# Reordering the third feed-forward ring and taking the best sums from four bands of candidates

## The chip, the cores and the metric

The kernel runs on one core of a Trainium2 chip. Its time is the device time of one execution in microseconds; lower is better. The engines are TensorE (PE, with its weight loads as PEld), VectorE (DVE), ScalarE (ACT), GpSimd (POOL) and SyncE (SP, which issues the transfers). Each has its own queue, in which instructions go in order; semaphores order work between queues.

## The reference

Four transformer layers, each an attention and a feed-forward part, over 2048 rows of width 128. The change touches the feed-forward part of the second layer, a lookup among experts by product keys:

```python
x = inputs.reshape(b * s, d)
xn = (x - x.mean(axis=0)) * rsqrt(x.var(axis=0) + EPS) * bn_gamma + bn_beta
q = (xn @ w_q.T).reshape(b, s, 2, NH, KD)...         # NH = 8 heads, KD = 128
sim = einsum('pbnhd,hkpd->pbnhk', q, keys_p)          # two lists of NK = 32 a head
scores, idx = top_k(sim, K)                           # K = 8 best of each list
all_scores = (scores[0][..., :, None] + scores[1][..., None, :]).reshape(..., K * K)
all_idx = ...
sc, pk = top_k(all_scores, K)                         # 8 best of 64 sums
indices = take_along_axis(all_idx, pk)
hmid = sigmoid(sc) * gelu(einsum('bnd,bnhkd->bnhk', inputs, down[indices]))
return einsum('bnhk,bnhkd->bnd', hmid, up[indices])
```

Both lists of eight are sorted, the largest first.

## The kernel before

The lookup is computed densely. There are 32 x 32 = 1024 possible experts, so for a tile of 128 rows and a head the kernel adds every similarity of list one to every one of list two (1024 sums), and keeps the sigmoid of a sum where the sum is at least the eighth best. These gates, turned and summed over the 8 heads, weight a dense product with all experts.

There are 16 tiles of 128 rows (`TILES`). Each passes through a ring over 8 heads, head h of tile i being step n = 8i + h:

- POOL, `pool1`: the 1024 sums of a head (`pairsum`, four buffers, so product n waits for gate n-4). Line 1669.
- ACT, `step` in `scalar1`: the sigmoid of the sums into PSUM (two buffers, `sig_bank`, so it waits for gate n-2). Line 1643. After the sigmoid of head 3 it does three other things for later tiles: `inputs` (the normalized rows of tile i+3), `copy_sims` (the similarities of tile i+2 out of PSUM, line 1625), `lowered` (gelu of the expert inputs of tile i+1 in two halves, line 1633, with a table load before and one after it).
- VectorE, `step` in `vector1`: the gate, `(pairsum >= eighth best) * sigmoid` (`gated`, four buffers, line 1741). In between: `mix` (turned gates times gelu, tile i-1, line 1726) after the gate of head 1, `tops` (16 MAX8 over 32 similarities, tile i+1, line 1701) after heads 2 and 3, `combine` (64 sums for each of 8 heads, one instruction, line 1706) and `add_tile` (line 1731) after head 3, `bests` (8 MAX8 over 64 sums, line 1717) after heads 5 and 6.
- TensorE, `step` in `tensor1`: 8 transposes of the gates of a head, summed over the heads in PSUM (line 1571). In between: `upper(i-1)` after head 0 (16 matrix products in the profile, line 1561), `similar(i+2)` after head 1 (line 1547), both halves of `lower(i+1)` after head 3 (line 1552).

`similar` and the first half of `lower` share bank 6, `upper` and the second half of `lower` share bank 7; the waits that this needs are in the code. `steps1` runs the tiles: the first four and the last four written out, the eight in the middle in a loop over groups of four. In the call of a step, `first` tells how many tiles came before and `last_` how many come after. `own_wait` is a memset of one element on VectorE.

Of the kernel before, what the change touches and what calls it, by code (L numbers as in the profile page):

```python
# [25 lines left out]
P = 128  # L26
# [3 lines left out]
TILES = TOKENS // P  # L30
# [1210 lines left out]
NE_USED = 1024  # L1241
CHUNKS = NE_USED // P
PK_HEADS, NK, TOPK = 8, 32, 8
EXPERTS = 8
CAPACITY = 640


def feed_forward(nc, ctx, sb, sem, S, w):
# [25 lines left out]
    xbT = QT[:, 2, :].rearrange("p (a b) -> p a b", a=2)  # L1274
    sims = OT[:].rearrange("p a b -> p (a b)").rearrange("p (g n) -> p g n", g=4)
    top = sb("top", [P, 2, 16, TOPK])
    combos = QT[:, 4:6, :].rearrange("p a b -> p (a b)")
    best = sb("best", [P, 2, PK_HEADS, TOPK])
    pairsum = KM[:].rearrange("p a b c -> p (a b c)").rearrange("p (r n) -> p r n", r=4)
    gated = both[:].rearrange("p (r n) -> p r n", r=4)  # L1280
# [252 lines left out]
    def tensor1(pe, A):  # L1533
# [31 lines left out]
        def step(first, last_, i, t):  # L1565
            for h in range(PK_HEADS):
                pe.wait_ge(gated_ready, PK_HEADS * i + h + 1)
                if h == 0 and first > 0:
                    pe.wait_ge(mixed, 2 * i)
                for c in range(CHUNKS):  # L1570
                    last = pe.matmul(weight_bank(c), gated[:, h % 4, c * P:(c + 1) * P], ident[:],  # L1571
                                     is_transpose=True, start=(h == 0 and c % 4 == 0),
                                     stop=(h == PK_HEADS - 1 and c % 4 == 3), skip_group_check=True)
                last.then_inc(wT_done, 1)
                if h == 0 and first > 0:

                    pe.wait_ge(act_ready[1], 2 * i + 2)
                    upper(i - 1, t - 1)
                if h == 1 and last_ > 1:

                    pe.wait_ge(act_ready[1], 2 * i + 1)
                    similar(i + 2, t)
                if h == 3 and last_ > 0:

                    if last_ > 1:
                        pe.wait_ge(sims_ready, i + 3)
                    lower(i + 1, 0)
                    if first > 0:
                        pe.wait_ge(added[1], i)
                    lower(i + 1, 1)  # L1590
# [7 lines left out]
        lower(0, 1)  # L1598
        steps1(pe, step)
        prepare_tensor(pe)  # L1600
        upper(TILES - 1, TPG - 1)
        prepare_tensor_end(pe)

    def scalar1(act, A):
# [31 lines left out]
        def step(first, last_, i, t):  # L1636
            for h in range(PK_HEADS):
                n = PK_HEADS * i + h
                act.wait_ge(sum_ready, n + 1)
                if first > 0 or h >= 2:  # L1640

                    act.wait_ge(gated_ready, n - 1)
                act.activation(sig_bank(h), pairsum[:, h % 4, :], ACT.Sigmoid).then_inc(sig_ready, 1)  # L1643
                if h == 3:
                    if last_ > 2:
                        inputs(first + 3, i + 3, t + 3)
                    if last_ > 1:
                        copy_sims(first + 2, i + 2, t + 2)
                    if last_ > 0:
                        lowered(first + 1, i + 1, t + 1)  # L1650

        inputs(0, 0, 0)
        inputs(1, 1, 1)
# [21 lines left out]
    def vector1(dve, A, before_last):  # L1675
# [27 lines left out]
        def combine(i, t):  # L1703
            dve.wait_ge(top_done, 16 * i + 16)
            pair = top[:, t % 2].rearrange("p (h q) k -> p h q k", q=2)
            dve.tensor_tensor(combos.rearrange("p (h a b) -> p h a b", h=PK_HEADS, a=TOPK),
                              pair[:, :, 0, :].unsqueeze(3).broadcast_to([P, PK_HEADS, TOPK, TOPK]),
                              pair[:, :, 1, :].unsqueeze(2).broadcast_to([P, PK_HEADS, TOPK, TOPK]), ALU.add)\
               .then_inc(combos_done, 1)

        def bests(i, t, lo, hi):

            if lo == 0:
                dve.wait_ge(combos_done, i + 1)
                S["own_wait"](dve, 1)
            for h in range(lo, hi):
                dve.max(best[:, t % 2, h, :], combos[:, h * 64:(h + 1) * 64]).then_inc(best_done, 1)

        def mix(i, t):

# [12 lines left out]
        def step(first, last_, i, t):  # L1733
            dve.wait_ge(best_done, PK_HEADS * i + PK_HEADS)
            for h in range(PK_HEADS):
                n = PK_HEADS * i + h
                dve.wait_ge(sig_ready, n + 1)
                if first > 0 or h >= 4:
                    dve.wait_ge(wT_done, n - 3)

                dve.scalar_tensor_tensor(out=gated[:, h % 4, :], in0=pairsum[:, h % 4, :],  # L1741
                                         scalar=best[:, t % 2, h, TOPK - 1:TOPK], in1=sig_bank(h),
                                         op0=ALU.is_ge, op1=ALU.mult).then_inc(gated_ready, 1)
                if h == 1 and first > 0:
                    mix(i - 1, t - 1)
                if last_ > 0:
                    if h == 2:
                        tops(i + 1, t + 1, 0, 8)
                    if h == 3:
                        tops(i + 1, t + 1, 8, 16)  # L1750
                        combine(i + 1, t + 1)
                    if h == 5:
                        bests(i + 1, t + 1, 0, 4)
                    if h == 6:
                        bests(i + 1, t + 1, 4, 8)
                if h == 3 and first > 0:
                    add_tile(i - 1)

        tops(0, 0, 0, 16)
        combine(0, 0)  # L1760
# [443 lines left out]
```

## Time and profile before

| | us |
|---|---|
| median of 3 runs | 1797.42 (1796.62 to 1799.19) |
| the profiled execution | 1804.69 |
| its span, first to last instruction | 1802.9 |
| PE busy | 1505.2 (83%) |
| DVE busy | 1081.5 (60%) |
| ACT busy | 897.9 (50%) |
| POOL busy | 714.2 (40%) |
| third feed-forward's ring, first product on POOL to the end of the last gate | 606.5 to 947.7 |

Busy shares are means over eight very different stages, of which the ring of the lookup is one. For that ring alone the stretches and the timeline have to be read. The granted clock of TensorE over the whole span is 0.927 of full speed.

### The profile page before, as it was taken

The page shows a single profiled execution, that of the slowest core. Times are in us where ns is not written, and L with a number is a line of the kernel's source. Part 1 is how long each engine was busy: PE and PEld are TensorE (multiplying, and loading weights), DVE is VectorE, ACT ScalarE, POOL GpSimd, SP SyncE. Part 2 cuts the span into 40 slices and gives each one's busy share as a digit, 9 for nine tenths or more (in the row PEclk, how much of TensorE's full clock was granted, in tenths as well). Part 3 has the DMA queues.
Part 4 walks back from the last instruction along what each step waited for, and adds up shares of the span by engine and source line. Part 5 has one row for each costly group of instructions (what it writes and reads, how often), then busy time and mean ns, then how long its engine had stood idle before and what let it go on. Part 6 is the DMA issues. An engine that isn't in the chain of part 4 may idle for free.

```text
span 1802.9 us, 28544 instructions
## 1 busy us (share of the span) xinstructions
PE 1505.2 (83%) x9457; PEld 956.4 (53%) x9457; DVE 1081.5 (60%) x2348; ACT 897.9 (50%) x1947; POOL 714.2 (40%) x1039
## 2 busy tenths in 40 slices
PE   5877689999998576666676888699989999997798
PEld 2434346666665366666663444344456666665343
DVE  4444447777776577677774554334367777766443
ACT  1333346666665466565561444333356666663222
POOL 5442124444443577677773333100034444433000
PEclk9999799999999689888886999889999999998899
DMA  1006000000000000000000000000000000000000
GB/s 60 13 16 259 1 4 4 6 3 3 3 3 1 0 1 1 1 1 0 1 1 7 7 7 7 4 21 1 3 3 4 3 3 3 3 0 1 1 12 12
DMA packets 13668, 21.72 MB, mean 12 GB/s; under 512 B 3200, under 2 KB 10256, under 8 KB 13072
## 3 DMA queue, kind: packets, MB, share of 16 engines
q1 hardware_dynamic: 13584, 20.63, 3.3%
q8 instruction: 49, 0.80, 0.2%
q14 instruction: 35, 0.29, 0.1%
HBM read 19.58 MB, written 1.05 MB: 11 GB/s over the span
## 4 chain that ended last, share of the span: by engine, by line
PE 58%; DVE 20%; ACT 10%; issue 6%; POOL 5%; DVEq 0%; ACTq 0%; DMA 0%; SPq 0%; POOLq 0%
DVE sb_VP L649 5%; PE bank L1571 5%; ACT sb_both L969 5%; PE bank L909 5%; PE bank L887 5%; PE bank L872 4%; PE bank L384 3%; DVE bank L1049 3%; POOL sb_QT L733 3%; PE bank L1962 3%; PE bank L860 3%; PE bank L1782 3%; DVE sb_both L1741 3%; PE bank L839 2%; DVE sb_wneg L1051 2%
## 5 line engine op out<-in xcount | busy, mean ns | idle before, releaser
L1117 POOL TENSOR_TENSOR sb_both<-sb_both,sb_winv 128x512 f32<-128x512 f32 x256 | 261.1, 1042 | 362.7 <-DVE sb_winv L1056 362.7
L1669 POOL TENSOR_TENSOR sb_KM<-sb_OT 128x1024 f32<-128x1024 f32 x128 | 247.4, 1973 | 95.4 <-DVE sb_both L1741 91.4
L1571 PE MATMUL bank<-sb_ident,sb_both 128*128 128x128 f32 x1024 | 161.7, 324 | 106.7 <-DVE sb_both L1741 71.7
L969 ACT ACTIVATE sb_both<-bank,sb_wneg 128x256 f32<-128x256 f32 x512 | 235.6, 475 | 29.3 <-DVE sb_wneg L1051 29.0
L1741 DVE SCALAR_TENSOR_TENSOR sb_both<-sb_KM,sb_best,bank 128x1024 f32<-128x1024 f32 x128 | 159.7, 1271 | 98.8 <-ACT bank L1643 98.4
L1571 PEld LDWEIGHTS bank<-sb_ident,sb_both 128*128 128x128 f32 x1024 | 147.4, 171 | 124.4 <-DVE sb_both L1741 78.7
L649 DVE TENSOR_REDUCE sb_VP<-bank 128x8 f32<-128x2048 f32 (+1 forms) x64 | 111.1, 1757 | 100.0 <-PE bank L390 100.0
L1051 DVE TENSOR_REDUCE sb_wneg<-bank 128x4 f32<-128x1024 f32 x128 | 156.7, 1224 | 4.4
L909 PE MATMUL bank<-sb_QT,sb_VP 128*64 128x256 f32 x1024 | 138.8, 392 | 19.0 <-DVE sb_QT L1063 13.3
L1643 ACT ACTIVATE bank<-sb_KM 128x1024 f32<-128x1024 f32 x128 | 130.3, 1026 | 47.7 <-DVE sb_both L1741 31.6
L872 PE MATMUL bank<-sb_KM 64*128 64x256 f32 x1024 | 145.2, 402 | 4.9 <-ACT sb_both L969 4.9
L1199 POOL TENSOR_TENSOR sb_ntmp<-sb_rstd 128x2 f32<-128x2 f32 (+2 forms) x123 | 24.3, 197 | 304.3 <-DVE sb_rstd L209 300.1
L887 PE MATMUL bank<-sb_ident,sb_both 128*128 128x128 f32 x1024 | 139.8, 279 | 0.0
L887 PEld LDWEIGHTS bank<-sb_ident,sb_both 128*128 128x128 f32 x1024 | 110.0, 141 | 48.7 <-issue 36.2
L872 PEld LDWEIGHTS bank<-sb_KM 64*128 64x128 f32 x1024 | 88.1, 186 | 69.4 <-issue 57.6
L955 ACT ACTIVATE sb_KM<-bank 128x512 f32<-128x512 f32 x128 | 77.1, 602 | 78.9 <-PE bank L840 78.2
L978 ACT ACTIVATE sb_QT<-bank 128x512 f32<-128x512 f32 x128 | 76.5, 598 | 78.6 <-PE bank L887 78.4
L969 ACT ACTIVATION_READ_ACCUMULATOR sb_both<-bank,sb_wneg 128x1 f32 x512 | 106.3, 208 | 0.0
L909 PEld LDWEIGHTS bank<-sb_QT,sb_VP 128*64 128x64 f32 x1024 | 62.6, 136 | 80.1 <-issue 34.7
L1056 DVE RECIPROCAL sb_winv<-sb_wsum 128x4 f32<-128x4 f32 x128 | 22.7, 177 | 135.3 <-ACT sb_both L969 135.3
L384 PE MATMUL bank<-sb_QT,sb_outT 32*128 32x512 f32 x384 | 61.4, 712 | 50.8 <-POOL sb_QT L733 29.6
L1063 DVE COPY sb_QT<-bank 128x512 f32<-128x512 f32 x128 | 87.4, 683 | 25.5 <-PE bank L887 25.0
(257 smaller groups left out, 2766.2 us busy)
## 6 DMA issues: line engine op xcount, KB each, us to landing
sb_ctxT_in<-in_ctxT SPq DMA_DIRECT2D x32, 128.0 KB, 2.3
sb_F<-in_F SPq DMA_DIRECT2D x2, 1024.0 KB
sb_XO<-in_ctx SPq DMA_DIRECT2D x8, 128.0 KB, 2.1
sb_WQ<-in_WQ SPq DMA_DIRECT2D x2, 512.0 KB, 5.8
sb_WK<-in_WK SPq DMA_DIRECT2D x2, 512.0 KB, 6.8
sb_WV<-in_WV SPq DMA_DIRECT2D x2, 512.0 KB, 7.6
sb_WO<-in_WO SPq DMA_DIRECT2D x2, 512.0 KB, 8.9
sb_WKQ<-in_WKQ SPq DMA_DIRECT2D x1, 1024.0 KB, 9.5
```

Of the source, the lines that this page charges most:

```text
L384: pe.matmul(bank[r][:], q[rows], keys, start=True, stop=False)
L649: last = dve.tensor_reduce(to, src, AX, ALU.max, negate=True)
L872: last = pe.matmul(s[:, h, i, :], QK[rows, t, 0, i * P:(i + 1) * P], QK[rows, t, 1, :], start=True, stop=True)
L887: last = pe.transpose(bank[4 + i][:, n * P:(n + 1) * P], PRW[:, t % 4, h, i, kt * P:(kt + 1) * P], ident[:])
L909: last = pe.matmul(bank[6][rows, 0:SEQ], VW[:, kt, (2 * t + h) * 64:(2 * t + h + 1) * 64], PTW[:, t % 2, h, kt, :], start=kt == 0, stop=kt ...
L969: last = act.activation(PRW[:, t % 4, h, i, :], s[:, h, i, :], ACT.Exp, bias=wneg[:, t % 4, h, i:i + 1], accum_out=wsum[:, t % 4, h, i:i + 1])
L1051: dve.tensor_reduce(wneg[:, t % 4], s, AX, ALU.max, negate=True).then_inc(w_neg, 1)
L1117: pool.tensor_tensor(p, p, winv[:, t % 4, :, i:i + 1].broadcast_to([P, 2, SEQ]), ALU.mult).then_inc(w_norm, 1)
L1571: last = pe.matmul(weight_bank(c), gated[:, h % 4, c * P:(c + 1) * P], ident[:], is_transpose=True, start=(h == 0 and c % 4 == 0), stop=(h ...
L1643: act.activation(sig_bank(h), pairsum[:, h % 4, :], ACT.Sigmoid).then_inc(sig_ready, 1)
L1669: pool.tensor_tensor(dst, s[:, h, 0, :].unsqueeze(2).broadcast_to([P, NK, NK]), s[:, h, 1, :].unsqueeze(1).broadcast_to([P, NK, NK]), ALU. ...
L1741: dve.scalar_tensor_tensor(out=gated[:, h % 4, :], in0=pairsum[:, h % 4, :], scalar=best[:, t % 2, h, TOPK - 1:TOPK], in1=sig_bank(h), op0 ...
```

## The change

At each step of the ring the work for other tiles is placed at other heads. TensorE: `similar(i+2)` and `upper(i-1)` both after head 0, in this order, the halves of `lower(i+1)` after head 1 and head 2. ACT: `inputs` after head 1, `copy_sims` after head 4, `lowered` after head 6. VectorE: `mix` after head 0; `add_tile`, all 16 `tops` and `combine` after head 4; `bests` stays after heads 5 and 6.

The eight best of the 64 sums of two sorted lists can only be among pairs (a, b) whose ranks, counted from one, multiply to at most 8. `combine` now writes four bands that cover these pairs: rank 0 of list one with the 8 best of list two, rank 1 with 4, ranks 2 and 3 with 2, ranks 4 to 7 with 1; 20 sums a head in place of 64. Each band is an instruction of its own over all 8 heads (64, 32, 32 and 32 elements a partition), and `bests` searches 20 elements.

```diff
--- before.py
+++ after.py
@@ -1241,6 +1241,8 @@
 NE_USED = 1024
 CHUNKS = NE_USED // P
 PK_HEADS, NK, TOPK = 8, 32, 8
+BANDS = ((0, 1, 8, 0), (1, 2, 4, 8), (2, 4, 2, 12), (4, 8, 1, 16))
+CANDIDATES = 20
 EXPERTS = 8
 CAPACITY = 640
 
@@ -1274,7 +1276,7 @@
     xbT = QT[:, 2, :].rearrange("p (a b) -> p a b", a=2)
     sims = OT[:].rearrange("p a b -> p (a b)").rearrange("p (g n) -> p g n", g=4)
     top = sb("top", [P, 2, 16, TOPK])
-    combos = QT[:, 4:6, :].rearrange("p a b -> p (a b)")
+    combos = QT[:, 4, 0:PK_HEADS * CANDIDATES].rearrange("p (h n) -> p h n", h=PK_HEADS)
     best = sb("best", [P, 2, PK_HEADS, TOPK])
     pairsum = KM[:].rearrange("p a b c -> p (a b c)").rearrange("p (r n) -> p r n", r=4)
     gated = both[:].rearrange("p (r n) -> p r n", r=4)
@@ -1572,19 +1574,17 @@
                                      is_transpose=True, start=(h == 0 and c % 4 == 0),
                                      stop=(h == PK_HEADS - 1 and c % 4 == 3), skip_group_check=True)
                 last.then_inc(wT_done, 1)
-                if h == 0 and first > 0:
-
+                if h == 0:
                     pe.wait_ge(act_ready[1], 2 * i + 2)
-                    upper(i - 1, t - 1)
-                if h == 1 and last_ > 1:
-
-                    pe.wait_ge(act_ready[1], 2 * i + 1)
-                    similar(i + 2, t)
-                if h == 3 and last_ > 0:
-
+                    if last_ > 1:
+                        similar(i + 2, t)
+                    if first > 0:
+                        upper(i - 1, t - 1)
+                if h == 1 and last_ > 0:
                     if last_ > 1:
                         pe.wait_ge(sims_ready, i + 3)
                     lower(i + 1, 0)
+                if h == 2 and last_ > 0:
                     if first > 0:
                         pe.wait_ge(added[1], i)
                     lower(i + 1, 1)
@@ -1598,6 +1598,7 @@
         lower(0, 1)
         steps1(pe, step)
         prepare_tensor(pe)
+        pe.wait_ge(added[1], TILES - 1)
         upper(TILES - 1, TPG - 1)
         prepare_tensor_end(pe)
 
@@ -1641,13 +1642,12 @@
 
                     act.wait_ge(gated_ready, n - 1)
                 act.activation(sig_bank(h), pairsum[:, h % 4, :], ACT.Sigmoid).then_inc(sig_ready, 1)
-                if h == 3:
-                    if last_ > 2:
-                        inputs(first + 3, i + 3, t + 3)
-                    if last_ > 1:
-                        copy_sims(first + 2, i + 2, t + 2)
-                    if last_ > 0:
-                        lowered(first + 1, i + 1, t + 1)
+                if h == 1 and last_ > 2:
+                    inputs(first + 3, i + 3, t + 3)
+                if h == 4 and last_ > 1:
+                    copy_sims(first + 2, i + 2, t + 2)
+                if h == 6 and last_ > 0:
+                    lowered(first + 1, i + 1, t + 1)
 
         inputs(0, 0, 0)
         inputs(1, 1, 1)
@@ -1703,18 +1703,19 @@
         def combine(i, t):
             dve.wait_ge(top_done, 16 * i + 16)
             pair = top[:, t % 2].rearrange("p (h q) k -> p h q k", q=2)
-            dve.tensor_tensor(combos.rearrange("p (h a b) -> p h a b", h=PK_HEADS, a=TOPK),
-                              pair[:, :, 0, :].unsqueeze(3).broadcast_to([P, PK_HEADS, TOPK, TOPK]),
-                              pair[:, :, 1, :].unsqueeze(2).broadcast_to([P, PK_HEADS, TOPK, TOPK]), ALU.add)\
-               .then_inc(combos_done, 1)
+            for lo, hi, n, at in BANDS:
+                dst = combos[:, :, at:at + (hi - lo) * n].rearrange("p h (a b) -> p h a b", b=n)
+                dve.tensor_tensor(dst, pair[:, :, 0, lo:hi].unsqueeze(3).broadcast_to([P, PK_HEADS, hi - lo, n]),
+                                  pair[:, :, 1, 0:n].unsqueeze(2).broadcast_to([P, PK_HEADS, hi - lo, n]), ALU.add)\
+                   .then_inc(combos_done, 1)
 
         def bests(i, t, lo, hi):
 
             if lo == 0:
-                dve.wait_ge(combos_done, i + 1)
+                dve.wait_ge(combos_done, len(BANDS) * (i + 1))
                 S["own_wait"](dve, 1)
             for h in range(lo, hi):
-                dve.max(best[:, t % 2, h, :], combos[:, h * 64:(h + 1) * 64]).then_inc(best_done, 1)
+                dve.max(best[:, t % 2, h, :], combos[:, h, :]).then_inc(best_done, 1)
 
         def mix(i, t):
 
@@ -1741,20 +1742,18 @@
                 dve.scalar_tensor_tensor(out=gated[:, h % 4, :], in0=pairsum[:, h % 4, :],
                                          scalar=best[:, t % 2, h, TOPK - 1:TOPK], in1=sig_bank(h),
                                          op0=ALU.is_ge, op1=ALU.mult).then_inc(gated_ready, 1)
-                if h == 1 and first > 0:
+                if h == 0 and first > 0:
                     mix(i - 1, t - 1)
-                if last_ > 0:
-                    if h == 2:
-                        tops(i + 1, t + 1, 0, 8)
-                    if h == 3:
-                        tops(i + 1, t + 1, 8, 16)
+                if h == 4:
+                    if first > 0:
+                        add_tile(i - 1)
+                    if last_ > 0:
+                        tops(i + 1, t + 1, 0, 16)
                         combine(i + 1, t + 1)
-                    if h == 5:
-                        bests(i + 1, t + 1, 0, 4)
-                    if h == 6:
-                        bests(i + 1, t + 1, 4, 8)
-                if h == 3 and first > 0:
-                    add_tile(i - 1)
+                if h == 5 and last_ > 0:
+                    bests(i + 1, t + 1, 0, 4)
+                if h == 6 and last_ > 0:
+                    bests(i + 1, t + 1, 4, 8)
 
         tops(0, 0, 0, 16)
         combine(0, 0)
```

## Rows read from the trace of the kernel before

**Rows 1.** Stretches: length, busy us (instructions) of PE, PEld, DVE, ACT, POOL, granted clock.

```profile
630.60:930.20 299.60, 205.38 (x1371) 190.14 (x1371) 212.99 (x533) 179.42 (x193) 216.41 (x112) 0.85 0.00 1
...
801.67:824.11 22.44, 16.12 (x99) 15.16 (x99) 15.16 (x39) 12.92 (x14) 15.46 (x8) 0.80 0.00 0
...
824.11:844.92 20.81, 13.75 (x99) 12.56 (x99) 15.16 (x39) 12.92 (x14) 15.46 (x9) 0.91 0.00 0
```

**Rows 2.** Waits from 630.6 to 930.2: us in total, times, longest.

```profile
DVE sb_both L1741 <- ACT bank L1643: 85.7, 14, 7.2
...
POOL sb_KM L1669 <- DVE sb_both L1741: 84.1, 14, 7.0
...
PE bank L1571 <- DVE sb_both L1741: 66.3, 19, 4.3
```

**Rows 3.** Timeline of tiles 8 and 9: start us, us, engine, line.

```profile
804.41 0.60 DVE L1717 MAX8 sb_best<-sb_QT 128x8 f32<-128x64 f32 x4
...
808.63 1.28 DVE L1726 TENSOR_TENSOR sb_xn_all<-bank,sb_xn_all 128x512 f32<-128x512 f32 x2
...
811.27 3.21 PE L1561 MATMUL bank<-sb_up,sb_xn_all 128*128 128x128 f32 x16
...
812.96 0.84 DVE L1701 MAX8 sb_top<-sb_OT 128x8 f32<-128x32 f32 x8
...
813.84 1.52 DVE L1706 TENSOR_TENSOR sb_QT<-sb_top 128x512 f32<-128x512 f32 x1
...
816.39 0.60 ACT L1625 ACTIVATE sb_OT<-bank 128x512 f32<-128x512 f32 x1 [5.71 <-PE bank L1547]
...
820.40 1.28 ACT L1643 ACT_TABLE_LOAD   x1
...
822.76 2.47 DVE L1741 SCALAR_TENSOR_TENSOR sb_both<-sb_KM,sb_best,bank 128x1024 f32<-128x1024 f32 x2 [7.20 <-ACT bank L1643]
...
824.11 15.46 POOL L1669 TENSOR_TENSOR sb_KM<-sb_OT 128x1024 f32<-128x1024 f32 x8 [6.98 <-DVE sb_both L1741]
```

**Rows 4.** Timeline: first gate of the ring, and the last mix.

```profile
615.90 3.72 DVE L1741 SCALAR_TENSOR_TENSOR sb_both<-sb_KM,sb_best,bank 128x1024 f32<-128x1024 f32 x3 [5.81 <-ACT bank L1643]
...
948.84 1.29 DVE L1726 TENSOR_TENSOR sb_xn_all<-bank,sb_xn_all 128x512 f32<-128x512 f32 x2 [1.19 <-PE bank L1571]
```

**Rows 5.** Timeline of TensorE at a granted clock of 1.00.

```profile
833.33 1.95 PE L1561 MATMUL bank<-sb_up,sb_xn_all 128*128 128x128 f32 x16
...
835.12 1.04 PE L1571 MATMUL bank<-sb_ident,sb_both 128*128 128x128 f32 x8
...
835.99 1.02 PE L1547 MATMUL bank<-sb_QT 128*128 128x512 f32 x2
```

**Rows 6.** Timeline of POOL around one combine, and in the last tile.

```profile
812.89 1.92 POOL L1669 TENSOR_TENSOR sb_KM<-sb_OT 128x1024 f32<-128x1024 f32 x1
...
814.76 2.38 POOL L1669 TENSOR_TENSOR sb_KM<-sb_OT 128x1024 f32<-128x1024 f32 x1
...
930.26 15.02 POOL L1669 TENSOR_TENSOR sb_KM<-sb_OT 128x1024 f32<-128x1024 f32 x8 [4.47 <-DVE sb_both L1741]
```

**Rows 7.** Line 1706: duration ns min/median/max.

```profile
L1706 DVE TENSOR_TENSOR sb_QT<-sb_top x16: 876/1525/1687, 608.1 to 922.3; 128x512 f32<-128x512 f32 x16
```

**Rows 8.** Timeline from 10.6 us: VectorE beside POOL.

```profile
10.10 0.92 POOL L733 TENSOR_SCALAR sb_QT<-sb_ctxT,sb_slabmask 128x256 f32<-128x256 f32 x1
...
10.71 0.33 DVE L203 TENSOR_SCALAR sb_veps<-sb_mv 128x2 f32<-128x2 f32 x1
...
10.78 0.27 DVE L204 TENSOR_SCALAR sb_vhalf<-sb_mv 128x2 f32<-128x2 f32 x1
```

**Rows 9.** Timeline of TensorE at the low clock.

```profile
609.22 3.60 PE L1552 MATMUL bank<-sb_xnT_all,sb_downT 128*128 128x128 f32 x16 [0.69 <-ACT sb_OT L1625]
...
617.24 3.67 PE L1571 MATMUL bank<-sb_ident,sb_both 128*128 128x128 f32 x16 [4.41 <-DVE sb_both L1741]
```

**Rows 10.** One stretch, columns as in rows 1.

```profile
801.00:805.00 4.00, 3.35 (x16) 3.35 (x17) 4.00 (x13) 2.75 (x4) 3.33 (x2) 0.50 0.00 0
```

## The prediction

> **What bounds the kernel now.** I first read the page and the stretches of the third feed-forward ring. Its 16 tiles take 340 us, and in the 14 middle ones (from the fifth gate of tile 0 to the fifth gate of tile 14) no engine is full: of 299.6 us POOL is busy 216.4, VectorE 213.0, TensorE 205.4 [rows 1]. That is 21.4 us a tile, of which VectorE needs 15.2 and POOL 15.46. Two single tiles there take 22.44 and 20.81 us with the same 15.16 and 15.46 us of VectorE and POOL; they differ in TensorE's granted clock, 0.80 against 0.91 [rows 1].
>
> The waits name the place: the gate waits 85.7 us for ACT's sigmoid, 14 times, and POOL waits 84.1 us for the gate [rows 2]. One long wait a tile, so I looked at the timeline of one tile [rows 3]. POOL runs eight products without a pause, having stood for 6.98 us before them. In the tile before, the best candidates are taken (804.41), then comes the product with the mixed weights (808.63), `upper` on TensorE (811.27), and only at 816.39, after 5.71 us of idling, can ACT copy the similarities of tile i+2. Behind that copy in ACT's queue stand a table load, two gelu copies, another table load (820.40), and then sigmoids 4 and 5. Gate 4 starts at 822.76 after 7.20 us. The ring holds two sigmoids and four products, so the 11 us that ACT is away from the ring (from 816.39-5.71 = 810.7 to 820.40+1.28 = 821.7) can't be covered. It is a chain of order, not of work.
>
> **The moves.** `similar(i+2)` now goes ahead of `upper(i-1)` at head 0, its copy is at head 4 and the gelu copies at head 6, where `lower` has been issued at heads 1 and 2. I follow one tile in VectorE's order, zero at the start of gate 5, with gates 1.2 us apart (2.47 for two [rows 3]): bests, gate 6, bests, gate 7, gate 0, mix, gates 1 to 4, add, 16 tops, bands. The mix, now one gate earlier, waits for the transposes of gate 7: in the last tile it starts 1.19 us after gate 7's end [rows 4], and gate 0 takes 1.2 in between, so this costs nothing at the high clock, 0.4 to 0.9 at the low one.
>
> TensorE at the high clock: 8 transposes 1.04 us, similar 1.02, upper (16 matmuls) 1.95, lower as long as that [rows 5]. Mix ends at about 6.9. Then T0, similar, upper, T1 end at 12.0; the copy of similarities needs sigmoid 4, hence gate 2, and ends at 11.1, so it is in time; lower half 0, T2, lower half 1 (it needs add_tile, behind gate 4, at 11.9) end at 15.0. Gate 6 of that tile starts at 18.0 and needs T2 (14.0); gate 7 at 19.5 needs T3 (16.0). TensorE isn't late.
>
> ACT: sigmoid 6 needs product 6 (12.6) and gate 4, ends at 13.7; table 1.28, gelu copies 0.6 each (as the copy at 816.39), table 1.28 [rows 3]: sigmoid 7 ends at 18.5, gate 7 wants it at 19.5. A slack of 1.0 on ACT, of 1.6 on lower half 1. Behind the waiting ACT stands only sigmoid 7. No DMA moves.
>
> So the long wait goes, and what is late next is VectorE together with POOL. POOL alone: the last tile, which has no combine, runs its eight products in 15.02 us, 1.88 each; those with a combine take 15.46 [rows 3, 6].
>
> **Bests.** Eight MAX8 over 64 elements cost 0.15 each (four in 0.60), over 32 elements 0.105 (eight in 0.84) [rows 3]. Over 20 I take 0.105: minus 0.36 us a tile. The bound on the other side, a cost by elements alone, would be 0.1 us more; it moves nothing.
>
> **The bands, the disputed price.** Now one instruction of 512 elements takes 0.88 to 1.69 us [rows 7], though the product of 512 with one input in PSUM takes 0.64 (the mix, two in 1.28 [rows 3]). Its length goes by POOL: the product before it ends at 814.81, the combine ends at 815.36 (813.84+1.52), 0.55 us behind, and the product after it takes 2.38 instead of 1.92 [rows 3, 6]. The spread of the 16 (876 to 1687 ns) is that of a wait for the boundary by how early each is issued. So this instruction, with two inputs in SBUF, gets in only between two POOL products, and the next one waits for it. Four bands (64, 32, 32, 32 elements) have four such entries. Unhindered they cost some 0.5 us (0.17 of streaming by 160/512 of 0.55, and 0.1 for each instruction more, as for a short MAX8). What does POOL do between them? At 10.7 us two tiny VectorE instructions that were both waiting end at 11.04 and 11.05, right behind the end of a POOL instruction at 11.02 and together [rows 8]: two that are waiting pass in one gap. Nothing here shows a third. The next product streams about 0.09 us after the boundary (0.55 minus the 0.46 by which it is lengthened), which is when two bands are through, so I take it that the product goes ahead of bands 3 and 4. Lower bound: all four in one gap, 0.5 us. Upper bound: a whole product between any two.
>
> The upper bound is cut by the ring. Product n+4 needs gate n, and gate 5 stands behind the bands; so, once gate 4 is done, at most the product five heads on stands open and POOL then has nothing to start. However the four are served, at most the rest of the current product and one more get ahead.
>
> The sum: from gate 5 to the bands VectorE has 15.16 minus 1.52 (combine) minus 0.36, 13.3 us. POOL, having run dry, restarts 1.35 after gate 5's start (822.76 to 824.11 [rows 3]) and has boundaries at 1.35+1.88k: 12.6, 14.5, 16.4. The bands are issued at 13.3, wait for 14.5, two pass, a product runs, two pass at 16.4 into an idle POOL. Gate 5 follows at 16.5. **16.5 us a tile against 21.4.** If the work ahead is up to 1.1 longer, the result is the same; 1.1 to 3.0 longer, the bands meet the last product, then an empty POOL: the same again.
>
> The Trainium skill ("SBUF — State Buffer", "Who interferes with whom" and "SBUF: two separate sides") says that the second port pair is shared by VectorE and GpSimd and locked for a whole instruction, also by a VectorE operation with two SBUF inputs against a GpSimd one that reads SBUF. The trace agrees, by the 0.55 and 0.46 us above. It speaks against splitting the combine; by it alone, a lock for each of four, the period is also 16.5, for the ring's reason.
>
> **Ends.** Gate 0 of tile 0 stays at 615.90 [rows 4]; the bands of tile 0's own lookup run while ACT is still at its first gelu copies. Gate 4 then ends at about 621.9 (at the low clock of that stretch still: it hangs on gates and sigmoids) instead of 630.6 [rows 1]: -8.7. From gate 4 of tile 14 to the last gate's end there were 17.4 us (930.2 to 948.84-1.19 = 947.65 [rows 1, 4]); now bands and a whole tile lie in it, 16.5+5.4 = 21.9: +4.5. Middle: 14 x (16.5-21.4) = -68.6. Sum -72.8 us. `wait added` ahead of the last `upper` costs nothing, the add was done a tile's half before. The profiled execution took 1804.69 us (span 1802.9, 1.8 around it), 7.3 over the median 1797.42; the difference of 72.8 taken off the median gives **1725 us**.
>
> **Rivals.**
> A. VectorE keeps its turn over all four bands, so POOL is the bound. For: the pair above passed together. Against: the pair was tiny and the next product no later than its own start. Bands at 14.5+0.3; product period 15.02+0.3 = 15.3; tail 20.9. 621.9+14x15.3+20.9 = 857, against 947.65: -90.6, 1707 us.
> B. TensorE's clock costs part of it. Low-clock rows: lower (upper the same) 3.60, transposes 1.84 a head (16 in 3.67) [rows 9], similar taken as twice its 1.02: 23.9 us a tile against 13.2 high, plus 1.4 of idling at the mix. At a mixture as now (some 0.85 granted, three tenths low) that is 17.8. For: the clock does fall inside the tiles, to 0.50 (1.2 GHz) in the stretch 801 to 805 [rows 10]. Against: that is right behind TensorE's stand of 4.3 us for gate 4 [rows 2], and this stop goes; 1.4 us is the longest left. With 18.0 us a tile: -51, 1746 us.
> C. Slower than before: the clock stays low all through the ring. 23.9+1.4 = 25.3 a tile: 14 x 3.9 = +55, ends a few us, 1852. It decides from the point where over 67% of TensorE's work is at the low clock (13.2+10.7s+1.4 = 21.7). A granted 0.80 to 0.91 is 20 to 40% of the time at the low level [rows 1].
> D. The moves free nothing, because the copy of the similarities at head 4 or the add at head 4 holds TensorE, which feeds the gates again: time as before. That would need TensorE 3 us later at T2 than I count.
>
> **How the numbers follow.** The forecast 56%, with its own range 1718 to 1735 (16.2 to 17.2 a tile); A 18%; B, with all between 17.2 and 19 a tile, 21%; C 3%; D 2%. The range 1704 to 1746 leaves out C, D and the slower half of B. 0.2% is 3.6 us, about what a measurement of this kernel can tell from no change. Faster 0.95, within 0.02, slower 0.03.
>
> **What would show it.** POOL: eight products with one pause of about 1.4 us a tile, not 6.0, and one or two longer products among them. Bands: the first ends just behind a boundary, the third or fourth nearly 2 us after it. Gate 5 starts right behind the fourth. No wait of the gate for ACT over 1 us. Granted clock above 0.9. It would be wrong if bands all end in one gap (A), if gates wait for transposes (B), or if gate 7 waits for its sigmoid by more than 1 us, which would put the bound on ACT's head 6.

## The result, and the profile after

The changed kernel takes 1729.89 us (median of 4 runs, 1728.46 to 1732.07), the kernel before beside it 1797.8. The ratio is 0.9625, interval 0.961 to 0.9639: 67.9 us less. The forecast was 1725.

The profiled execution spans 1726.7 us. Of its page, the groups of POOL's products and of the gates (now line 1742): name and shapes, count, busy us and mean ns, idle us before them and what ended the idling.

```profile
L1669 POOL TENSOR_TENSOR sb_KM<-sb_OT 128x1024 f32<-128x1024 f32 x128 | 240.1, 1912 | 31.4 <-DVE sb_both L1742 27.4
...
L1742 DVE SCALAR_TENSOR_TENSOR sb_both<-sb_KM,sb_best,bank 128x1024 f32<-128x1024 f32 x128 | 158.5, 1274 | 10.2 <-ACT bank L1644 10.2
```

The gates wait 10.2 us for ACT in the whole ring (85.7 in its 14 middle tiles before [rows 2]), POOL 27.4 us for the gates.

The ring's stretches, columns as in [rows 1]: 14 tiles, then one tile at the high and one with a part at the low clock.

```profile
627.20:860.00 232.80, 180.83 (x1371) 159.75 (x1371) 219.01 (x576) 175.07 (x194) 210.09 (x113) 0.95 0.00 1
...
777.00:793.50 16.50, 12.27 (x99) 10.85 (x99) 15.80 (x42) 12.47 (x15) 14.97 (x9) 1.00 0.00 0
...
694.00:710.70 16.70, 13.67 (x99) 12.02 (x99) 15.31 (x43) 12.61 (x14) 15.01 (x8) 0.90 0.00 1
```

Of the 14 tiles, 13 take 16.5 to 16.7 us against the 20.8 and 22.4 of the two in [rows 1]; one takes 17.1, where the mix waits 0.70 us for transposes (649.24). VectorE is shown busy for 15.8 of 16.5 us, but that counts the time in which a band waits for its turn beside POOL, so VectorE isn't full of work. The granted clock went from 0.85 to 0.95. The waits from 627 to 860 us, as in [rows 2]:

```profile
POOL sb_KM L1669 <- DVE sb_both L1742: 24.2, 16, 1.7
...
ACT L1644 <- DVE sb_both L1742: 22.1, 15, 1.8
...
DVE sb_both L1742 <- ACT bank L1644: 8.1, 14, 0.6
...
DVE sb_x L1732 <- PE bank L1563: 3.8, 6, 0.8
```

The timeline of one tile, which answers to [rows 3]:

```profile
760.41 1.28 ACT L1644 ACT_TABLE_LOAD   x1 [1.81 <-DVE sb_both L1742]
...
760.42 15.01 POOL L1669 TENSOR_TENSOR sb_KM<-sb_OT 128x1024 f32<-128x1024 f32 x8 [1.53 <-DVE sb_both L1742]
...
762.77 2.47 DVE L1742 SCALAR_TENSOR_TENSOR sb_both<-sb_KM,sb_best,bank 128x1024 f32<-128x1024 f32 x2 [0.57 <-ACT bank L1644]
...
768.48 1.95 PE L1563 MATMUL bank<-sb_up,sb_xn_all 128*128 128x128 f32 x16
...
771.36 0.28 DVE L1732 TENSOR_TENSOR sb_x<-bank,sb_x 128x128 f32 x1
...
773.19 2.49 DVE L1708 TENSOR_TENSOR sb_QT<-sb_top 128x64 f32<-128x64 f32 x4
...
775.60 1.27 DVE L1742 SCALAR_TENSOR_TENSOR sb_both<-sb_KM,sb_best,bank 128x1024 f32<-128x1024 f32 x1
...
776.95 15.01 POOL L1669 TENSOR_TENSOR sb_KM<-sb_OT 128x1024 f32<-128x1024 f32 x8 [1.52 <-DVE sb_both L1742]
```

Eight products run in 15.01 us, then POOL stands for 1.5 us until gate 5 (775.60) is done: 760.42 to 776.95 is 16.53 us. `upper` (768.48) is done before gate 4 ends, so add_tile (771.36) has no wait. In front of gate 7 (762.77) stand 0.57 us for its sigmoid. The four bands take 2.49 us together; unhindered, one of 32 elements takes 0.18. One by one, with the product that runs beside them:

```profile
773.19 0.45 DVE L1708 TENSOR_TENSOR sb_QT<-sb_top 128x64 f32<-128x64 f32 x1
...
773.51 1.92 POOL L1669 TENSOR_TENSOR sb_KM<-sb_OT 128x1024 f32<-128x1024 f32 x1
...
773.56 1.92 DVE L1708 TENSOR_TENSOR sb_QT<-sb_top 128x32 f32<-128x32 f32 x1
...
775.40 0.28 DVE L1708 TENSOR_TENSOR sb_QT<-sb_top 128x32 f32<-128x32 f32 x2
```

Band 1 ends at 773.64, right behind the product's end at 773.56. Band 2 starts at 773.56 and ends at 775.48: the next product (773.51, 1.92 us) has gone ahead of it. A band starts only some 0.08 us before the one ahead of it ends, and by then the next product is there. Bands 3 and 4 pass right behind band 2, since POOL then has nothing to start. In tile 0, where POOL still has open products, even those wait one by one:

```profile
607.57 1.91 DVE L1708 TENSOR_TENSOR sb_QT<-sb_top 128x32 f32<-128x32 f32 x1
...
609.40 1.94 DVE L1708 TENSOR_TENSOR sb_QT<-sb_top 128x32 f32<-128x32 f32 x1
...
611.26 1.94 DVE L1708 TENSOR_TENSOR sb_QT<-sb_top 128x32 f32<-128x32 f32 x1
```

Of the 15 tiles in which the bands of the next one are computed, nine go as in the timeline above. In the other six, all with a clock of 0.90, band 1 comes just too late for the end of a product:

```profile
707.59 1.85 DVE L1708 TENSOR_TENSOR sb_QT<-sb_top 128x64 f32<-128x64 f32 x4
...
707.59 1.55 DVE L1708 TENSOR_TENSOR sb_QT<-sb_top 128x64 f32<-128x64 f32 x1
```

Here it is band 1 that takes 1.55 us, waiting for the last product, and the other three pass into an idle POOL. They are the six tiles in which add_tile waits for `upper` (the last row of the waits, 3.8 us in all, 0.8 at most); POOL's pause is 1.66 us in place of 1.52 and the tile 16.66 in place of 16.53, so a missed end costs 0.13 us more than a second band held up.

The last gate ends at 875.50:

```profile
874.22 1.28 DVE L1742 SCALAR_TENSOR_TENSOR sb_both<-sb_KM,sb_best,bank 128x1024 f32<-128x1024 f32 x1 [0.59 <-ACT bank L1644]
```

The ring, from POOL's first product (605.66) to there, takes 269.8 us against 341.2.

### The profile page after: what moved, and what is told of

Read it like the earlier page. It is cut to its first block, busy times and chain, and to the rows that moved or that the text cites. A ratio compares the mean times of both kernels' runs of the same rounds, so it can differ in the third digit from the quotient of the medians.

```text
span 1726.7 us, 28570 instructions
## 1 busy us (share of the span) xinstructions
PE 1472.2 (85%) x9445; PEld 923.3 (53%) x9457; DVE 1094.5 (63%) x2396; ACT 892.7 (52%) x1947; POOL 705.5 (41%) x1039
## 4 chain that ended last, share of the span: by engine, by line
PE 52%; DVE 25%; ACT 9%; issue 7%; POOL 5%; DVEq 0%; ACTq 0%; DMA 0%; SPq 0%; POOLq 0%
DVE sb_VP L649 6%; ACT sb_both L969 5%; PE bank L909 5%; PE bank L887 5%; PE bank L872 4%; DVE sb_both L1742 4%; PE bank L384 3%; DVE bank L1049 3%; POOL sb_QT L733 3%; PE bank L1781 3%; PE bank L860 3%; PE bank L1961 3%; PE bank L839 3%; DVE sb_wneg L1051 2%; PE bank L390 2%
## 5 line engine op out<-in xcount | busy, mean ns | idle before, releaser
L1669 POOL TENSOR_TENSOR sb_KM<-sb_OT 128x1024 f32<-128x1024 f32 x128 | 240.1, 1912 | 31.4 <-DVE sb_both L1742 27.4
L1573 PE MATMUL bank<-sb_ident,sb_both 128*128 128x128 f32 x1024 | 141.6, 288 | 60.1 <-DVE sb_both L1742 37.7
L1742 DVE SCALAR_TENSOR_TENSOR sb_both<-sb_KM,sb_best,bank 128x1024 f32<-128x1024 f32 x128 | 158.5, 1274 | 10.2 <-ACT bank L1644 10.2
L1573 PEld LDWEIGHTS bank<-sb_ident,sb_both 128*128 128x128 f32 x1024 | 120.2, 148 | 75.5 <-DVE sb_both L1742 49.2
L887 PE MATMUL bank<-sb_ident,sb_both 128*128 128x128 f32 x1024 | 139.8, 280 | 0.0
L887 PEld LDWEIGHTS bank<-sb_ident,sb_both 128*128 128x128 f32 x1024 | 110.0, 141 | 48.7 <-issue 36.2
```

The costliest lines, as they stand in the source:

```text
L887: last = pe.transpose(bank[4 + i][:, n * P:(n + 1) * P], PRW[:, t % 4, h, i, kt * P:(kt + 1) * P], ident[:])
L1669: pool.tensor_tensor(dst, s[:, h, 0, :].unsqueeze(2).broadcast_to([P, NK, NK]), s[:, h, 1, :].unsqueeze(1).broadcast_to([P, NK, NK]), ALU. ...
```

## The experiments

Ratios are to the kernel before, run beside them on the same chip. Its own median was 1797.8 to 1801.2 us in these groups of runs (0.2% apart), so the ratios are what to compare.

**Moves alone.** One instruction of 64 sums as before, all placements as in the changed kernel.

```diff
-            for lo, hi, n, at in BANDS:
-                dst = combos[:, :, at:at + (hi - lo) * n]...
-                dve.tensor_tensor(dst, ..., ALU.add).then_inc(combos_done, 1)
+            dve.tensor_tensor(combos.rearrange("p (h a b) -> p h a b", h=PK_HEADS, a=TOPK), ...)\
+               .then_inc(combos_done, 1)
```

> The moves as in the changed kernel, but the 64 sums in one instruction and the bests over 64, as before. Theory T (turns): a VectorE instruction with two inputs in SBUF and a POOL product exclude each other, and POOL's next product goes ahead of the second such instruction; in the changed kernel a tile therefore pays the rest of one product, a whole product, and POOL's pause of 1.5 us. One instruction pays the rest of a product only, ends 0.55 us behind the boundary, and lengthens the next product by 0.46, so that POOL never runs dry: 15.5 us a tile (8 x 1.88 + 0.46), 14 tiles x 1.05 = 15 us under the changed kernel, about 1715 us, ratio to the kernel before about 0.954. POOL's pauses are gone or under 0.3 us. Rival R (VectorE's own work and ACT's order set the period, the lock costs little): one instruction of 64 sums and the longer bests are 0.9 to 1.4 us a tile more work, so the time is 1735 to 1745 us.

Measured 1716.27 us, ratio 0.9543 (0.9526 to 0.956): faster than the changed kernel by 0.8%, some 15 us, the intervals apart. POOL's products:

```profile
643.36 15.01 POOL L1669 TENSOR_TENSOR sb_KM<-sb_OT 128x1024 f32<-128x1024 f32 x8 [1.82 <-DVE sb_both L1741]
...
660.19 15.01 POOL L1669 TENSOR_TENSOR sb_KM<-sb_OT 128x1024 f32<-128x1024 f32 x8 [1.81 <-DVE sb_both L1741]
...
693.83 167.34 POOL L1669 TENSOR_TENSOR sb_KM<-sb_OT 128x1024 f32<-128x1024 f32 x87 [1.82 <-DVE sb_both L1741]
```

The last row is 87 products in 167.34 us without a pause, 15.4 us a tile: POOL is the bound. But four earlier tiles have a pause of 1.8 us, which the expectation did not hold. The combine and the gate behind it, in the good part:

```profile
767.82 1.38 DVE L1706 TENSOR_TENSOR sb_QT<-sb_top 128x512 f32<-128x512 f32 x1
...
769.13 1.27 DVE L1741 SCALAR_TENSOR_TENSOR sb_both<-sb_KM,sb_best,bank 128x1024 f32<-128x1024 f32 x1
```

It is issued at 767.82, gets in at the end of the product at 768.7 and is done at 769.20; nothing else has to get in. Theory T stands for these tiles and R falls: more work in one instruction is faster than less work in four. In the four tiles with a pause T fails, which the last experiment looks into.

**No combine.** The sums of the best candidates are left out, so the thresholds, and with them the result, are not those of the lookup; everything else is as in the changed kernel.

```diff
-            for lo, hi, n, at in BANDS: ...
+            dve.nop().then_inc(combos_done, len(BANDS))
```

> The changed kernel without any combine: the sums of the best candidates are left out, the search for the best reads what lies there. Theory T: POOL is the bound, 15.0 us a tile and no pause, 22 us under the changed kernel, about 1708 us (ratio 0.950). Rival R: VectorE's work from gate 5 to gate 5 is 13.3 plus 0.57 of waiting for the sigmoid of head 7, plus the wait for the next product; if something else than the lock holds the period (gate 7's wait, TensorE), it stays above 16 us, 1720 or more.

Measured 1709.55 us, 0.9498 (0.9475 to 0.9522). POOL mostly runs through two tiles at a time:

```profile
646.00 29.98 POOL L1669 TENSOR_TENSOR sb_KM<-sb_OT 128x1024 f32<-128x1024 f32 x16 [0.57 <-DVE sb_both L1738]
```

The 14 middle tiles take 15.4 us each on average, not the 15.0 without a pause that theory T had: POOL still pauses 0.4 to 0.6 us for a gate in about every second tile, and once 1.4. But without the bands nothing else holds the period at 16.5. The four bands, half a microsecond of work by the estimate, cost 1.3% of the kernel by the ratios; the ring of the profile is 19.7 us shorter without them (250.1 against 269.8).

**Two bands.** 28 sums in two instructions.

```diff
-BANDS = ((0, 1, 8, 0), (1, 2, 4, 8), (2, 4, 2, 12), (4, 8, 1, 16))
-CANDIDATES = 20
+BANDS = ((0, 2, 8, 0), (2, 8, 2, 16))
+CANDIDATES = 28
```

> The changed kernel with two bands in place of four: ranks 0 and 1 with 8 each, ranks 2 to 7 with 2 each, 28 sums in two instructions. Theory T: the first passes at a boundary, a product goes ahead of the second, POOL then stands: 16.5 to 16.6 us a tile, as with four, within 3 us of the changed kernel (1727 to 1733). Rival R (each instruction has its price, 0.1 us and its share of waiting): two fewer give 0.2 us a tile or more; if turns cost a product for each, two fewer would give nothing either, since the ring is empty. If two waiting instructions pass in one gap, as at 10.7 us in the trace of before, there is no pause and it takes 1708 to 1715.

Measured 1730.77 us, 0.9628 (0.9608 to 0.9649), the same as four. The second instruction lets the product go ahead, the third and fourth cost nothing more:

```profile
755.40 2.41 DVE L1708 TENSOR_TENSOR sb_QT<-sb_top 128x128 f32<-128x128 f32 x2
...
759.08 15.01 POOL L1669 TENSOR_TENSOR sb_KM<-sb_OT 128x1024 f32<-128x1024 f32 x8 [1.39 <-DVE sb_both L1742]
```

**Gelu copies at head 5.**

```diff
-                if h == 6 and last_ > 0:
+                if h == 5 and last_ > 0:
                     lowered(first + 1, i + 1, t + 1)
```

> The changed kernel with ACT's gelu copies of tile i+1 after the sigmoid of head 5 instead of 6. In the changed kernel the table load for sigmoid 7 starts only when gate 5 is done, and gate 7 waits 0.57 us for it. Theory T: the wait is hidden, since the bands wait for a product's end anyway: 16.53 us a tile, within 3 us of the changed kernel, at most 0.05 us a tile better where the bands now miss a boundary. Rival R: gate 7's wait is on the path, 0.57 x 15 = 8.5 us better, 1721 us.

Measured 1730.88 us, 0.9624 (0.9606 to 0.9643): no difference. In the tile shown gate 7 has no wait now (762.02), the bands are issued 0.7 us earlier in the beat than in the changed kernel and take that much longer (3.16 for 2.49), and POOL starts again after 16.52 us (three of the 14 middle tiles take 16.8 to 17.0):

```profile
760.32 15.00 POOL L1669 TENSOR_TENSOR sb_KM<-sb_OT 128x1024 f32<-128x1024 f32 x8 [1.52 <-DVE sb_both L1742]
...
762.02 2.45 DVE L1742 SCALAR_TENSOR_TENSOR sb_both<-sb_KM,sb_best,bank 128x1024 f32<-128x1024 f32 x2
...
772.41 3.16 DVE L1708 TENSOR_TENSOR sb_QT<-sb_top 128x64 f32<-128x64 f32 x4
...
776.84 1.91 POOL L1669 TENSOR_TENSOR sb_KM<-sb_OT 128x1024 f32<-128x1024 f32 x1 [1.52 <-DVE sb_both L1742]
```

A wait in front of the gates was on the engine that sets the period and still cost nothing, since what follows waits for POOL's boundary.

**Bands alone.** The kernel before, its order untouched, with the four bands.

> The kernel before with the four bands and the bests over 20 and nothing moved. The bands stand behind gate 3, in front of the long wait for ACT (7.2 us), where VectorE has time. Theory T: the bands' wait for a product goes into that wait; the bests behind gates 5 and 6 are on VectorE's path, 0.36 us a tile, which TensorE's path at the low clock can eat: 0 to 5 us better, 1793 to 1798 us, ratio 0.997 to 1.000. Rival R (the bands cost time where they stand, up to 2 us a tile): 1800 to 1828 us. Either way the bands bring none of the change's 68 us, and the moves all of it.

Measured 1797.36 us against 1800.48, 0.9976 (0.9965 to 0.9988), 12 runs. The bands take 3.30 us, all of it within the long wait for the sigmoid:

```profile
812.52 3.30 DVE L1710 TENSOR_TENSOR sb_QT<-sb_top 128x64 f32<-128x64 f32 x4
...
820.24 2.47 DVE L1744 SCALAR_TENSOR_TENSOR sb_both<-sb_KM,sb_best,bank 128x1024 f32<-128x1024 f32 x2 [4.22 <-ACT bank L1645]
...
821.60 1.91 POOL L1671 TENSOR_TENSOR sb_KM<-sb_OT 128x1024 f32<-128x1024 f32 x1 [6.03 <-DVE sb_both L1744]
```

So the moves bring all of the gain and more: 0.9543 alone, 0.9625 with the bands. The bands, with the shorter search that comes with them, bring 0.24% where the ring waits for something else, and take 0.8% where it doesn't. The moves were tried as a whole; apart from the gelu copies (above) and the mix (below), which of them does how much was not tested.

**All 64 sums in two halves.** As moves alone, but four heads in each of two instructions: the same work, one entry more.

```diff
-            dve.tensor_tensor(combos..., PK_HEADS heads, ALU.add).then_inc(combos_done, 1)
+            for lo in (0, 4):
+                dve.tensor_tensor(sums[:, lo:lo + 4], ..., 4 heads, ALU.add).then_inc(combos_done, 1)
```

> The moves with all 64 sums, computed in two instructions of four heads each instead of one. Against moves alone only the number of instructions differs, not the work. Theory T: the first half ends some 0.3 us behind a boundary, a product goes ahead of the second, POOL runs dry in every tile: 16.6 to 17.0 us a tile, 1733 to 1740 us. Rival (size decides, or two waiting instructions pass in one gap): as moves alone, 1716 to 1720 us.

Measured 1737.25 us, 0.9646 (0.9623 to 0.967), against 0.9543 for one instruction: 1.0%, 18 us, for one more instruction. That is a little more than the 16.6 to 17.0 us a tile that were expected: the 14 middle tiles take 17.1 on average. The pair takes 2.70 us, and POOL's pause is back:

```profile
760.61 2.70 DVE L1708 TENSOR_TENSOR sb_QT<-sb_top 128x256 f32<-128x256 f32 x2
...
763.23 1.27 DVE L1743 SCALAR_TENSOR_TENSOR sb_both<-sb_KM,sb_best,bank 128x1024 f32<-128x1024 f32 x1
...
764.58 15.19 POOL L1669 TENSOR_TENSOR sb_KM<-sb_OT 128x1024 f32<-128x1024 f32 x8 [1.55 <-DVE sb_both L1743]
```

**Mix behind gate 1.**

```diff
-                if h == 0 and first > 0:
+                if h == 1 and first > 0:
                     mix(i - 1, t - 1)
```

> The changed kernel with the mix put back behind gate 1. The transposes of head 0, similar, upper and lower start 1.2 us later. Theory T: TensorE has 1.6 us of room there, so the period stays at 16.5 to 16.7 us: 1727 to 1734 us. Rival (TensorE's chain is on the path, the mix had to move too): 1.2 x 15 = 18 us more, 1748 us.

Measured 1738.56 us, 0.9656 (0.9633 to 0.9679), by the ratios some 5 us slower than the changed kernel, though the two intervals still overlap by a little: neither the nothing that was expected nor the 18 us of the rival. The trace has 17.0 us a tile on average where the changed kernel has 16.7. The waits from 627 to 860, and the add in one tile:

```profile
DVE sb_x L1732 <- PE bank L1563: 25.4, 14, 2.9
...
PE bank L1573 <- DVE sb_xn_all L1727: 36.8, 14, 2.6
```

```profile
690.89 0.29 DVE L1732 TENSOR_TENSOR sb_x<-bank,sb_x 128x128 f32 x1 [1.98 <-PE bank L1563]
```

In this tile TensorE stands 2.63 us for the mix, `upper` then takes 2.92 us instead of the 1.95 of the high clock, and add_tile, which stands ahead of the tops on VectorE, waits 1.98 us for it. That the add hangs on `upper` was in no term of mine. It is 17.0 us a tile and not 17.7 (16.5 and the 1.2 of the rival), since the bands then find POOL empty: in most tiles the four take 0.5 to 0.7 us.

**Moves alone, gelu copies at head 5.**

> The moves with one instruction of 64 sums, and the gelu copies after the sigmoid of head 5. With the moves alone POOL ran dry in four tiles (pauses of 1.82 us) and then never again. Theory T: whether POOL runs dry hangs on whether the combine is issued before or after the end of the next to last open product; gate 7's wait for its sigmoid (0.21 to 0.57 us) lies ahead of it on VectorE. Without this wait the combine is earlier, the four pauses go, 4 x 1.4 = 5.6 us: 1710 to 1713 us, ratio about 0.951. Rival: the four pauses come from TensorE's clock in the first tiles, and stay: 1716 us.

Measured 1737.27 us, 0.9649 (0.9629 to 0.9668): a miss by 25 us, and the wrong way. ACT and the gate in one tile, then a stretch of two tiles:

```profile
758.64 0.60 ACT L1634 ACTIVATE sb_xn_all<-bank 128x512 f32<-128x512 f32 x1 [0.52 <-PE bank L1554]
...
759.26 1.28 ACT L1644 ACT_TABLE_LOAD   x1
...
760.56 1.97 ACT L1644 ACTIVATE bank<-sb_KM 128x1024 f32<-128x1024 f32 x2
...
761.62 1.28 DVE L1741 SCALAR_TENSOR_TENSOR sb_both<-sb_KM,sb_best,bank 128x1024 f32<-128x1024 f32 x1 [0.99 <-ACT bank L1644]
```

```profile
710.30:744.50 34.20, 26.81 (x198) 23.61 (x197) 30.65 (x78) 25.46 (x29) 30.55 (x16) 0.90 0.01 1
```

Sigmoid 6 now stands behind the gelu copies: the second waits 0.52 us for `lower`, the table load follows, and gate 6 waits 0.99 us for it. The stretch of two tiles gives 17.1 us a tile at a clock of 0.90, but the two are unlike: in the middle of the ring they take 15.7 and 18.5 us by turns. POOL pauses 1.8 us behind every second combine and 0.4 to 0.7 us behind gates in between, and the mix waits 0.97 us for transposes at the low clock (766.75). In the changed kernel a wait in front of a gate disappeared in the wait for POOL's boundary; here it doesn't. Which of these waits the 20 us come from was not separated.

**Moves alone, add_tile behind the tops**, and the moves alone once more beside it.

```diff
+                    if last_ > 0:
+                        tops(i + 1, t + 1, 0, 16)
                     if first > 0:
                         add_tile(i - 1)
                     if last_ > 0:
-                        tops(i + 1, t + 1, 0, 16)
                         combine(i + 1, t + 1)
```

The reason for it, in the first run of the moves alone: a tile that runs dry and one that doesn't (stretches), and the add and the combine of the dry one (timeline).

```profile
660.20:677.00 16.80, 13.80 (x100) 11.99 (x99) 15.80 (x39) 12.68 (x14) 14.99 (x8) 0.90 0.01 1
...
740.00:755.40 15.40, 12.29 (x100) 10.87 (x99) 15.06 (x39) 12.49 (x15) 15.40 (x9) 1.00 0.00 0
```

```profile
671.87 0.29 DVE L1731 TENSOR_TENSOR sb_x<-bank,sb_x 128x128 f32<-128x128 f32 x1 [0.76 <-PE bank L1563]
...
673.71 2.03 DVE L1706 TENSOR_TENSOR sb_QT<-sb_top 128x512 f32<-128x512 f32 x1
```

> The moves with one instruction of 64 sums, and add_tile behind the 16 tops instead of ahead of them. In the moves alone four early tiles ran dry (16.8 us, clock 0.90) and all later ones not (15.4 us, 1.00). Theory L (a loop): POOL dry makes TensorE stand, the clock falls, upper is late, add_tile holds VectorE 0.74 us for it, the combine misses the end of the next to last open product, and POOL is dry again. With add_tile behind the tops its wait is covered by them: the dry tiles go, up to 4 x 1.4 = 5.6 us, 1711 to 1714 us on a chip where the moves alone take 1716, and 0.996 to 0.998 of them. Rival: add_tile's wait is no part of it, or lower half 1, which waits for it 1.7 us longer, makes TensorE late: the same or slower, with the four dry tiles still there.

> The moves alone once more, beside the one with add_tile later, on the same chip: ratio to the kernel before 0.953 to 0.956 as in its first run, four or so dry tiles with a pause of 1.8 us on POOL and 15.4 us a tile in the rest. If the state of the ring hangs on chance at its start, the number of dry tiles differs from the four of the first run.

Measured 1713.76 us, 0.9508 (0.9491 to 0.9525), beside 1716.2 us, 0.9529 (0.9513 to 0.9546), for the moves alone, which had the same four dry tiles as at first. The dry tiles are gone; POOL runs all products but the first four in one piece:

```profile
615.25 238.77 POOL L1669 TENSOR_TENSOR sb_KM<-sb_OT 128x1024 f32<-128x1024 f32 x124 [2.66 <-DVE sb_both L1741]
```

That is the fastest version here, 1.2% under the changed kernel by the ratios. (The version without a combine, at 0.9498, leaves out part of the work.) Its lead over the moves alone is within what was expected, but the two intervals overlap; the missing pauses are what is sure. They are gone although the clock still falls: two tiles that follow each other take the same 15.4 us at 1.00 and at 0.89.

```profile
642.40:657.80 15.40, 12.75 (x104) 11.35 (x103) 14.84 (x39) 12.86 (x16) 15.40 (x9) 1.00 0.00 2
657.80:673.20 15.40, 13.01 (x97) 11.62 (x96) 15.18 (x38) 12.35 (x14) 15.40 (x9) 0.89 0.01 2
```

Six of the 14 middle tiles have the lower one. So the low clock needs no pause of POOL, and costs nothing where add_tile isn't held up by it: no add waits in these tiles.

## Why the prediction was right

The mechanism, its place and its size were as forecast, but for one step, which was wrong at no cost. Step by step:

- **The long wait goes.** It does: the gates' wait for ACT fell from 85.7 us [rows 2] to 8.1 in that part. What is left is 0.57 us a tile in front of gate 7.
- **16.5 us a tile, set by the bands and POOL in turn.** Measured 16.53 and, in tiles with some low clock, 16.66. POOL's pause was forecast as about 1.4 us and is 1.52. No combine and one instruction both bring POOL back as the bound, so the price is that of the entries, not of the gates' own work. The Trainium skill ("SBUF — State Buffer", "Who interferes with whom") has a VectorE instruction with two SBUF inputs and a GpSimd one that reads SBUF contend for a shared port, held for a whole instruction. The traces agree: in all six versions with more than one such instruction, each one that was issued during a product ended 0.04 to 0.28 us behind a product's end.
- **Two bands pass in one gap.** This step was wrong. One passes; the product goes ahead of band 2, not of band 3. The pair at 10.7 us [rows 8] did not carry over to the bands. Its two instructions were of another kind, with one tensor as input, and the second was issued (10.78) while the first still waited; band 2 starts when band 1 is nearly done, and the product has started 0.05 us before it. The wrong step cost nothing, for the reason given for the upper bound: after one more product the ring is empty. Tile 0, where it isn't, shows a whole product between any two. So the 16.5 us rest on that bound and would have come out with either order, by the prediction's own argument.
- **A longer product.** One of the signs was one or two lengthened products a tile. There are none: all 128 take 1.91 to 1.92 us. A combine of 512 elements ends 0.55 us behind the product's end and lengthens the next one by 0.46; band 1 ends only 0.08 behind it.
- **Slack.** I gave VectorE 1.1 us before it would miss the boundary. A wait that I had not seen took 0.57 of it: the table load in front of sigmoid 7 starts only when gate 5 releases that sigmoid (760.41, after 1.81 us of idling), so gate 7 waits 0.57 us. What was left was 0.3 us (773.19 to 773.51). In the six tiles where the add waits for `upper` it wasn't enough, and the case of the longer work ahead came in: band 1 meets the last product, the others an empty POOL, 16.66 us. Moving the load took the wait away and not a microsecond of time.
- **The mix and TensorE.** The mix at head 0 cost nothing at the high clock, as said, but its move seems worth more than I thought: without it `upper` is late for add_tile (some 5 us, with intervals that overlap a little).
- **Rival A** (the bands keep their turn) would have been 1707; the nearest runs, no combine and one instruction, are at 1710 and 1716. **Rival B**, the clock, is there in small, 0.13 us in the tiles at 0.90, and by another way than the sum of TensorE's work: through the add that waits for `upper`. The argument against it, that the clock fell behind a stand of 4.3 us that would go, holds in part: the clock rose from 0.85 to 0.95, but it still falls in some tiles, although TensorE waits at most 2.1 us for a gate there. **C** and **D** did not come.
- **The sum.** Up to the end of gate 4 in tile 0, -8.7 us were forecast and -8.7 measured (24.1 to 15.4 from the first product). For the 14 tiles it was -68.6 against -66.2 (299.5 to 233.3: 16.67 a tile in place of 16.5, by the six tiles and the one of 17.1), and for the rest +4.5 against +3.6 (17.5 to 21.1). Together -72.8 was forecast for the ring, and -71.3 measured. The medians differ by 67.9. The 3.4 us between are outside the ring or in the difference of single profiled executions. That of the kernel before was 7 us over its median and that of the changed one 1.4 under it; outside the ring the second was 4.9 us shorter. Two profiles don't settle which.

## What to carry to other kernels

When two engines take turns at something, count the entries and not the work: one instruction of 512 elements was cheaper than four with 160, because each further one lets a whole product of the other engine go first while that engine has one ready. A single entry that misses its turn costs as much, so what stands ahead of it counts too. A stage that waits long for one thing hides this; after the wait is removed, every cheap edit in it has to be priced again.

A wait costs nothing while its engine has to wait for a beat behind it anyway, and can cost a lot once the beat is gone. The same edit, the gelu copies one head earlier, gave nothing in one version and cost some 20 us in the next.

## What the runs showed of the hardware that was not expected

- VectorE instructions with two inputs in SBUF and POOL's products alternate as long as POOL has a product ready: the product starts a little before the second such instruction (773.51 and 773.56), which is then held to the product's end (775.48). This is so in all of the six versions with more than one, also for 32 elements, which take 0.18 us with POOL idle. The wait is shown as busy time of VectorE, not as idle time.
- In the moves alone, POOL's pause and TensorE's clock went together: 0.90 of full speed in each of the four dry tiles, 1.00 in the tiles at 15.4 us but one. With add_tile behind the tops they don't: no pause, and still 0.89 in six tiles. What the low clock does is to make `upper` late (in a tile of the changed kernel the 8 transposes ahead of it take 1.97 us at 683.65, against 1.09 at 766.69, and `similar` 1.54 against 1.02); the add waits 0.74 to 0.80 us for it in the four dry tiles, and the combine misses the product's end. Why the clock falls in some tiles and not in others, and why the run of dry tiles ends by itself after four, stays open.
